# A transformer block in fp32 on one core: layer 2's probabilities from one exponential instead of two, rounded on VectorE and split on GpSimd

## The reference, cut to what matters

```python
x = rmsnorm(hidden, ln1_w)
scores = q @ k.T / sqrt(32), causal                 # per batch, 16 heads
probs = softmax(scores);  attn = (probs @ v) @ Wo.T
mod = 0.1 * tanh(attn @ A)
gate = silu(h @ W_in.T + mod * (h @ A) @ B);  out = hidden + (gate * up) @ W_down.T
```

## Time and profile before

| | |
|---|---|
| median of three runs | 2788.23 us |
| the profiled execution | 2783.5 us, span 2781.7 us |
| busy in the span | TensorE 94%, VectorE 57%, ScalarE 48%, GpSimd 24% |
| TensorE in 900 to 1100 us (layer 2's attention) | 185.92 of 200 us busy, granted clock 1.00 |
| VectorE, ScalarE, GpSimd in the same stretch | 157.71, 132.03, 52.38 us |

### The profile page before, as it was taken

The page is one execution under the profiler, slowest core; times in us unless marked ns, Lnnn a source line. Parts: engine busy times, 40 slices in busy tenths (PEclk is TensorE's granted clock), DMA queues, the critical chain, the costliest instruction groups (busy, mean ns, idle before and its releaser), DMA issues.

```text
span 2781.7 us, 40963 instructions
## 1 busy us (share of the span) xinstructions
PE 2626.3 (94%) x13584; PEld 2016.5 (72%) x13584; DVE 1598.4 (57%) x4345; ACT 1327.0 (48%) x2739; POOL 661.8 (24%) x531
## 2 busy tenths in 40 slices
PE   7999999999878999999999889999999999999998
PEld 5777777777556667666666647888888888888886
DVE  6777777777747778788787774222222433333333
ACT  4777777777724666666666674111111321111111
POOL 4555565566321222222222221000000000000000
PEclk9999999999879999999999979999999999999999
DMA  6566666665635664555554544111111311111100
GB/s 153 113 142 145 148 131 141 146 142 128 159 97 121 127 128 109 128 129 110 129 132 103 129 84 162 47 47 47 47 47 47 115 47 47 47 47 47 47 30 31
DMA packets 174634, 276.44 MB, mean 99 GB/s; under 512 B 29556, under 2 KB 53876, under 8 KB 173940
## 3 DMA queue, kind: packets, MB, share of 16 engines
q1 hardware_dynamic: 171508, 260.57, 39.5%
q0 software_dynamic: 2304, 12.58, 1.3%
q10 hardware_dynamic: 640, 1.05, 0.1%
HBM read 97.03 MB, written 42.99 MB: 50 GB/s over the span
## 4 chain that ended last, share of the span: by engine, by line
PE 54%; DVE 9%; issue 3%; DMA 2%; ACT 2%; SPq 1%; POOL 1%; DVEq 0%; ACTq 0%; POOLq 0%
PE b_lin_ps L2542 13%; PE b_scores_ps L2553 13%; PE b_pv_ps L2523 6%; PE b_scores_t_ps L2523 6%; PE b_lin_ps L2071 5%; PE b_pv_ps L309 2%; DVE b_prob L292 2%; DVE b_junk L204 2%; PE b_scores_t_ps L273 2%; PE b_lin_ps L2034 2%; PE b_scores_ps L190 2%; DMA b_k_stack<-b_k_split 1%; PE b_lin_ps L2548 1%; PE b_scores_ps L2018 1%; ACT b_scores_t_ps L285 1%
## 5 line engine op out<-in xcount | busy, mean ns | idle before, releaser
L292 DVE TENSOR_TENSOR a_prob<-a_scores_t_ps,a_prob 128x384 fp32r<-128x384 f32 (+1 forms) x384 | 225.4, 593 | 139.1 <-ACT a_scores_t_ps L285 137.6
L284 ACT ACTIVATE b_prob<-b_scores_t_ps 128x384 fp32r<-128x384 f32 (+1 forms) x384 | 201.5, 525 | 215.2 <-PE b_scores_t_ps L275 194.8
L292 DVE TENSOR_TENSOR b_prob<-b_scores_t_ps,b_prob 128x384 fp32r<-128x384 f32 (+1 forms) x384 | 226.1, 593 | 102.4 <-ACT b_scores_t_ps L285 101.9
L284 ACT ACTIVATE a_prob<-a_scores_t_ps 128x384 fp32r<-128x384 f32 (+1 forms) x384 | 202.0, 526 | 154.8 <-PE a_scores_t_ps L275 129.9
L309 PE MATMUL a_pv_ps<-a_prob,a_value 128*65 128x512 f32 (+3 forms) x1024 | 273.4, 336 | 0.2 <-DVE a_prob L292 0.2
L309 PE MATMUL b_pv_ps<-b_prob,b_value 128*33 128x512 f32 (+3 forms) x1024 | 271.1, 333 | 0.2 <-DVE b_prob L292 0.2
L204 DVE CUSTOM_DVE_ANT_0 b_junk<-b_scores_ps,spare 128x512 bf16<-128x512 f32 (+3 forms) x512 | 226.8, 483 | 61.1 <-PE b_scores_ps L190 59.1
L204 DVE CUSTOM_DVE_ANT_0 a_junk<-a_scores_ps,spare 128x512 bf16<-128x512 f32 (+3 forms) x512 | 226.6, 483 | 24.8 <-PE a_scores_ps L190 22.7
L2486 DVE TENSOR_TENSOR b_res<-b_scores_ps,b_first_gate 128x512 f32<-128x512 f32 x64 | 44.2, 691 | 331.5 <-PE b_scores_ps L2553 331.5
L2486 DVE TENSOR_TENSOR stage<-b_scores_ps,b_junk 128x512 f32<-128x512 f32 x64 | 44.3, 692 | 327.9 <-PE b_scores_ps L2553 327.9
L1117 PE MATMUL a_lin_ps<-x_split,w_split 128*128 128x512 f32 x768 | 216.8, 397 | 1.3 <-DVE w_split L911 1.0
(11 more groups left out here) (315 smaller groups left out, 5897.4 us busy)
## 6 DMA issues: line engine op xcount, KB each, us to landing
a_q_stack<-a_q_split SPq DMA_DIRECT2D x192, 128.0 KB, 3.6
a_k_stack<-a_k_split SPq DMA_DIRECT2D x192, 128.0 KB, 3.6
b_q_stack<-b_q_split SPq DMA_DIRECT2D x192, 128.0 KB, 3.2
b_k_stack<-b_k_split SPq DMA_DIRECT2D x192, 128.0 KB, 3.7
spare<-h_t SPq DMA_DIRECT2D x16, 1024.0 KB, 6.2
stage<-in_x_t SPq DMA_DIRECT2D x8, 1024.0 KB, 6.4
a_sum_hi<-a_pv_raw SPq DMA_DIRECT2D x32, 256.0 KB, 3.8
spare<-a_pv_raw SPq DMA_DIRECT2D x32, 256.0 KB, 4.0
```

The lines of the kernel that those rows point to most:

```text
L284: act.activation(at.prob_hi[:, k % at.ring, 0:w], at.scores_t_ps[:, k % 2, 0:w], ACT.Exp, scale=SCALE)
L292: dve.tensor_tensor(at.prob_lo[:, k % at.ring, 0:w], at.scores_t_ps[:, k % 2, 0:w], at.prob_hi[:, k % at.ring, 0:w], ALU.subtract).then_in ...
```

## The change

ScalarE writes one exponential, in fp32, to SBUF (`exp_once`). VectorE copies it with rounding into `prob_hi` (`hi_unit`, in the place of `lo_unit`). GpSimd subtracts (`rest_unit`, at the head of its new slots). The fp32 tiles alternate between the MLP's first gate buffer and a slice of a shared buffer.

TensorE's `score_t_unit(k)` now waits for the exponential of unit k-2. `pv_unit` does its hi passes first, behind `hi_done`, and its lo passes behind `lo_done`. `exp_once(k)` waits for `lo_done` of unit k-2, whose fp32 tile it writes over.

`attn_chunk` and GpSimd's half of the normalised rows move to VectorE: the chunks go to slots 4 to 7 of group 3, rows 2 and 3 to slot 0 of group 2. GpSimd's program gets the slots of the others: `rest_unit` of the unit before in each, `merge` in slot 5, `adapter` in slot 7, and `weigh` in slot 9 of group 0 and slot 10 of the other groups.

```diff
-    at_least(pe, at.lo_done, n * UNITS + k - 1)
+    at_least(pe, at.exp_done if at.hi_done else at.lo_done, n * UNITS + k - 1)
...
+def exp_once(act, at, b, g, k):
+    u, w = number(b, g) * UNITS + k, WIDTH[k % 3]
+    act.wait_ge(at.score_t_ready, u + 1)
+    at_least(act, at.pv_done, u + 1 - at.ring)
+    at_least(act, at.lo_done, u - 1)
...
+    act.activation(exponentials(at, b, g, k)[:, 0:w], at.scores_t_ps[:, k % 2, 0:w], ACT.Exp,
+                   scale=SCALE).then_inc(at.exp_done, 1)
+def hi_unit(dve, at, b, g, k):
+    dve.wait_ge(at.exp_done, u + 1)
+    dve.tensor_copy(at.prob_hi[:, k % at.ring, 0:w], exponentials(at, b, g, k)[:, 0:w]).then_inc(at.hi_done, 1)
+def rest_unit(pool, at, b, g, k):
+    pool.wait_ge(at.hi_done, u + 1)
+    pool.tensor_tensor(at.prob_lo[:, k % at.ring, 0:w], exponentials(at, b, g, k)[:, 0:w],
+                       at.prob_hi[:, k % at.ring, 0:w], ALU.subtract).then_inc(at.lo_done, 1)
...
-    pv = PV_PASSES[j]
+    pv = sorted(PV_PASSES[j], key=lambda p: p[3]) if at.hi_done else PV_PASSES[j]
-            pe.wait_ge(at.lo_done, n * UNITS + k + 1)
+            pe.wait_ge(at.hi_done if at.hi_done else at.lo_done, n * UNITS + k + 1)
+        if at.hi_done and (kt, col, width, part) == next(p for p in pv if p[3] == 1):
+            pe.wait_ge(at.lo_done, n * UNITS + k + 1)
...
+            def step(b, g):                                   # GpSimd
+                for slot in range(UNITS):
+                    if slot > 0:
+                        rest_unit(pool, at, b, g, slot - 1)
+                    elif not first:
+                        rest_unit(pool, at, *group(b, g, -1), UNITS - 1)
+                    if slot == 5 and not first:
+                        merge(*group(b, g, -1))
...
+                    if slot == (9 if g == 0 else 10) and not first:
+                        weigh(*group(b, g, -1))
...
-                    exp_unit(act, at, b, g, slot)
+                    exp_once(act, at, b, g, slot)
-                        lo_unit(dve, at, b, g, slot - 1)
+                        hi_unit(dve, at, b, g, slot - 1)
+                    if g == 3 and 4 <= slot < 4 + KC and has(b, 2):
+                        attn_chunk(b + 2, slot - 4)
+                        if slot == 0:                         # VectorE, group 2
+                            h_rows(b + 1, 2)
+                            h_rows(b + 1, 3)
```

More of the change, by code:

```diff
@@ L1365, in gate_layer @@
         h_ready = sem("h_ready")
-        h_late = sem("h_late")
         h_turned = sem("h_turned")
@@ L1482, in step @@
                     sp.wait_ge(at.score_read, BATCH * GROUPS * UNITS)
+                    sp.wait_ge(at.lo_done, (BATCH * GROUPS - 1) * UNITS)
                     mlp.load_h(sp, mlp.start, 0)
@@ L1593, in _ @@
             pool.memset(at.value[:, :, :, 2 * RANK:2 * RANK + 1].bitcast(F32), 1.0).then_inc(at.ones_set, 1)
[L1594 to L1598, removed]
-            adapter(1)
[L1601 to L1606, removed]
+            adapter(1)
+            def step(b, g):
+                last = is_last(b)
+                first = isinstance(b, int) and b == 0 and g == 0
+                for slot in range(UNITS):
[5 more added lines that the diff above has]
+                        merge(*group(b, g, -1))
+                    if slot == 7 and last and g == 0:
                         pool.wait_ge(x1_out, BATCH * 16)
@@ L1611, in body @@
                             mlp.load_weights(pool, k)
-                    if is_last(b) and g == 2:
+                    if slot == 3 and last and g == 2:
                         for pair in range(2):
                             pool.wait_ge(at.stacked[pair], BATCH * GROUPS * 96)
+                        pool.wait_ge(at.lo_done, (BATCH * GROUPS - 2) * UNITS + 3)
                         mlp.clear(pool)
[L1616 to L1620, removed]
+                        pool.wait_ge(rows_zeroed, zeroed_before + 4)
+                    if slot == 7 and g == 3 and has(b, 2):
                         adapter(b + 2)
-                    if not (isinstance(b, int) and b == 0 and g == 0):
+                    if slot == (9 if g == 0 else 10) and not first:
                         weigh(*group(b, g, -1))
+            def body(b):
+                for g in range(GROUPS):
+                    step(b, g)
             batches(pool, body, 2)
+            rest_unit(pool, at, BATCH - 1, GROUPS - 1, UNITS - 1)
             for k in range(2, 4):
@@ L1758, in step @@
                         projected(*to)
+            act.wait_ge(both.attn_out, BATCH * GROUPS * 16)
             low_a_hi()
@@ L1784, in _ @@
             pv_copy(act, at, BATCH - 1, GROUPS - 1, 3)
+            act.wait_ge(at.lo_done, BATCH * GROUPS * UNITS)
             mlp.activations(act, lambda: tanh(BATCH - 1), lambda: z_part(BATCH - 1))
@@ L1805, in value_weights_lo, with attn_chunk @@
                                              op1=ALU.subtract).then_inc(w_ready, 1)
+            def attn_chunk(b, c):
+                dve.wait_ge(attn_hi, (b - 1) * KC + c + 1)
+                dve.tensor_tensor(attn_split[:, 1, c, :], wide[:, c, :], attn_split[:, 0, c, :],
+                                  ALU.subtract).then_inc(attn_ready, 1)
             def low(b):
@@ L1966, in _ @@
             dve.wait_ge(vw_made, 2)
-            for t in range(2):
+            for t in range(TT):
                 h_rows(0, t)
@@ L1986, in _ @@
             projected(0, 1, 1)
+            for c in range(KC):
+                attn_chunk(1, c)
             low(1)
```

32 lines of the change are left out of this document (17 added, 15 removed).

## The result

The changed kernel takes 2889.03 us (median of 4 runs, 2885.84 to 2890.48) against 2786.74 us before (4 runs): a ratio of 1.0367 (95% interval 1.0354 to 1.038), 3.7% slower. The forecast was 2836 us, in a range up to 2872: the sign was right, the loss came out twice as large, and the time lies outside the range. The profiled execution of the changed kernel took 2885.84 us, with a span of 2884.1 us, 102.4 us more than the span of before.

A forecast was written before the change was run, and what follows sets the result against it. TensorE was taken to set the pace, VectorE the only other engine near its limit. Terms 19 + 3 + 12 + 19 + 4 - 3 - 4 = 50 us on 2783.5 gave 2833.5, set midway 2836 us; range 2772 to 2872.

The forecast's parts named there:

- term 4: Group 1 slot 10 to group 2 slot 3: held and added VectorE work delays TensorE, 2.7 x 7 = 19 us.
- terms 1 to 3: Rests queued behind `weigh` delay TensorE: group 0 slot 9, 19 us; group 2 slot 10, 3; group 3 slot 10, 12.
- The port: Within SBUF, a GpSimd operation holds certain VectorE operations until it ends; without it, group 1 to 2 gains 2 to 3 us.
- term 5: Group 3, slots 4 to 8: four chunks and a collision against eight shorter copies on VectorE, 0.6 x 6 = 4 us.
- term 6: Other slots: waits on ScalarE return 0.4 x 7 = 3 us; last batch, with half of 11.4 us returning: -4.
- the third rival: VectorE becomes the bound: bunched copies each wait for a whole rest, TensorE's clock may drop; 2878 us, chance 0.15.
- the wait in slot 11 of group 0: Sign: TensorE's longest new wait on GpSimd's `prob_lo`, about 3 us, would stand there.
- the root operations of about 1 us: Sign: VectorE's root chain would show these where 0.17 us was usual, each ending with a GpSimd operation.
- the waits for rests: Sign: TensorE's new waits before its lo passes on GpSimd's `prob_lo`, about 8 us a batch.

The follow-up runs named there:

- weigh_in_pieces: The changed kernel with `weigh` cut into its two to four operations, one a slot behind that slot's rest: 2861.98 us, ratio 1.0268.
- moves_only: The changed kernel with ScalarE's two exponentials and VectorE's subtraction from PSUM put back, no rests on GpSimd, moved work kept: 2808.53 us, ratio 1.0072.
- two_exps_in_sbuf: The kernel before with the fp32 exponential in SBUF and hi passes first; both exponentials kept, VectorE subtracts, GpSimd as before: 2810.02 us, ratio 1.0079.
- filled_waits: The changed kernel plus 6 unused TensorE matmuls a batch in slots 0 and 1 of group 2: 2883.24 us, ratio 1.0347.
- unused rests: moves_only plus a GpSimd subtraction after each VectorE one, on a tile nobody reads, not in the last group: 2836.58 us, ratio 1.0176.

## Why the prediction was right in its sign and wrong in its size

The waits below are TensorE's, added up by slot from its timeline and averaged over the six batches. They cover 96.2 of its 101.0 us of idle time there, and 43.7 of 46.2 in the kernel before. One line of the kernel before that term 4 needs, from the same batch as the earlier trace rows:

```profile
1007.44 0.45 PE L273 MATMUL b_scores_t_ps<-b_q_stack,b_k_stack 114*128 114x256 f32 x2 [0.69 <-DVE b_prob L292]
```

- **GpSimd's queue (terms 1 to 3): right.** Slots 9 to 11 of group 0 wait 3.4 us a batch, where no wait stood (priced 2.7; slot 11 of the batch shown 3.12, walked 3.3). Around the start of group 3 it is 2.5 where 1.4 stood before, 1.1 more for 0.4 priced; I had not found the wait at 1047.26. At the batch's end it is 2.1 where 0.5 stood, 1.6 more for 1.7. weigh_in_pieces returned 28 us of a priced 34.
- **The port (term 4): right in kind, and near in size.** From slot 10 of group 1 to slot 3 of group 2 TensorE waits 4.2 us a batch (0.85 + 0.71 + 1.78 + 0.78 in the one shown). The kernel before has 2.1 us there, 1.41 and 0.69 (the line above), so it is 2.1 more, for 2.7 priced. Missed was how far the port reaches: VectorE's busy time in the six batches rose by 10.7 us, where I had -51 x 6/8 = -38. The casts take 0.53 us on average (199 us over 378 casts), not 0.38.
- **Group 3 (term 5): mis-sized.** Priced at 0.6 us a batch, although its own terms (2.7 of chunks less 1.7) give 1.0 before any collision. It is 2.8 where 0.7 stood, 2.1 more. moves_only, which has no rests, waits 3.0 us there, so it is the moved work and not the rests that costs this.
- **The other slots (term 6): right in sign, too small.** Priced at -0.4 us a batch, measured -1.5 (1.1 where 2.6 stood). The reason that I gave is not what the runs show: ScalarE itself now stands for rests (218.7 us over its five groups), and two_exps_in_sbuf shows that the 49.8 us of the earlier trace rows were mostly VectorE's lateness, which the next waits inherit.
- **The clock: no term at all. This is the step that failed.** The sum adds waits and takes TensorE's busy time as unchanged; I had left a lower clock to the third rival. It came behind the stretch in which TensorE was busy 1.38 of 4 us, with a mean idle share of 14% (101.0 of 703.2 us), and the kernel before had shown it in its last batch already (0.79). TensorE's busy time grew by 4.2 us a batch, 25 in six. How much of that would come back with the clock is open: filled_waits hardly restored it.
- **The last batch (term 6): wrong in sign.** Priced at -4, measured +11.3. GpSimd is busy 61.51 of its 83.66 us, and TensorE waits 21.8 us there for rests, 5.07 of them at 1691.45 for a rest behind a whole `weigh`, where it had waited 11.0 us for VectorE.

Added up by stretches, the forecast's shortfall of 52 us is 25 of busy time at the lower clock, 15 in the last batch, some 9 of idle time in the six batches (9.1 a batch for 7.7 summed), and the rest in the first batch and the MLP. That terms 1 to 6 come to 8.8 us a batch against 7.7 is partly luck: terms 1, 2 and 5 were priced too low, term 4 too high, and term 6 returned more than priced, and these errors offset each other. Of the signs that the prediction names, the wait in slot 11 of group 0 and the root operations of about 1 us came as said; the waits for rests are 13 us a batch (103.8 / 8), not 8, and a batch takes 117 us, not 110.

The third rival had nearly the right time (2878 us) and the lower clock, but not for its reason: VectorE did not become the bound. It was busy 146.03 of 200 us in the changed kernel, less than the 157.71 of the earlier trace rows.

By runs instead of by places, the 102 us are 20 for the moves, 29 for unused rests on GpSimd, and 53 for the dependence on them (difference of ratios; part of it would be larger but for the work that was saved). None of the parts alone is nearly all, and no version built here beats the kernel before.

## What to carry to other kernels

A half-busy engine isn't free room: price its new operations by what queues behind them, by the ring of buffers they hold, and by every operation that they hold on the engine beside them. A wait that vanishes from the list has to be followed to what was late behind it; if that engine has not become faster, the wait can reappear under another name, as it did in two_exps_in_sbuf. Where stalls of a few us are added, write a term for TensorE's clock as well, with a range from zero to the whole growth of its busy time, since no run here fixes its price.

## What the runs showed of the hardware that was not expected

- GpSimd's subtraction with both sources the same tile as its output took 1.057 us for 512 columns and 0.851 for 384; with a second source in another tile 1.305 and 1.036 (means from 900 to 1500 us).
- Halving its columns took it from 1.045 to 0.625 us, so some 0.2 us of a rest doesn't scale with the columns (2 x 0.625 - 1.045).
- ScalarE's exponential costs the same into SBUF as into PSUM: 0.490 and 0.598 us for 384 and 512 columns, against 0.487 and 0.595.
- VectorE's operations of 8 columns in SBUF were stretched from 0.17 to 1.26 us beside GpSimd, its subtractions from PSUM not at all (0.592 us with and without unused rests).
